# Delta rule: chunk queries and keys weighed together on GpSimd, moments of the outputs on ScalarE

## The chip, the cores and the metric

The kernel runs on one core of a Trainium2 chip. The metric is the time of one execution in microseconds (us) on the device. The engines are TensorE (PE, its weight loads are shown apart as PEld), VectorE (DVE), ScalarE (ACT), GpSimd (POOL) and SyncE (SP), which issues DMAs. Each runs its own list of instructions in order, and they wait for each other through counted semaphores. [...]

## The reference

Four blocks in a row work on x of 8 sequences, 512 tokens and 128 channels, each as x = x + block(layernorm(x)): an attention, an expert layer, the delta rule, and the expert layer again. The change is in the delta rule only:

```python
def step(S, inp):
    qt, kt, vt, at, gkt = inp
    Sp = S * jnp.exp(gkt)[..., None]
    u = jnp.einsum('bhk,bhkv->bhv', at, Sp) + vt
    S = Sp + jnp.einsum('bhk,bhv->bhkv', kt, u)
    o = jnp.einsum('bhk,bhkv->bhv', qt, S)
    return (S, o)
...
out = dplr_delta_rule(q, k, v, a, gk)      # a = k * gamma * exp(gk)
gate = jax.nn.sigmoid(x @ Wg1 @ Wg2)
out = out * gate
mu = jnp.mean(out, axis=-1, keepdims=True)
var = jnp.mean(jnp.square(out - mu), axis=-1, keepdims=True)
out = (out - mu) * jax.lax.rsqrt(var + 1e-05) * norm_w
return out @ Wo
```

There are 16 heads of 8 channels, so 8 sequences times 16 heads are 128 independent recurrences, one per partition.

## The kernel before

The delta rule has four stages on the time axis.

1. Projections (up to about 682 us in the profile): q, k, v, the decay and the gates are made and laid out with one head of one sequence per partition. `Q`, `K`, `V` and `W` are SBUF tiles of 128 x 4096 float32, in the order channel d, place j in the chunk, chunk c. A chunk is `CH` = 8 tokens, and there are `NCH` = 64 chunks. So two neighbouring places of one chunk lie 64 elements (256 bytes) apart, and two channels 512 elements.
2. Tables (about 682 to 758 us): for all chunks at once, VectorE multiplies (`product`), TensorE sums over the channels with an identity matrix (`sums`), and VectorE puts the lower triangular systems together in `LL` and `QQ`. Each product has one of four buffers, so `product(g)` waits for the sums of piece g-4. In between VectorE weighs all keys at once, W = K * beta (L2133), and at the end ScalarE replaces K by the keys that carry a token's part to the end of its chunk (L1933).
3. Recurrence (about 758 to 956 us): 64 chunks one after the other. Per chunk VectorE does four operations, each needing the one before it: the products of the state S with the weighted keys `w_c` (L2198, 128x512), their sum X (L2205), the products of X with the carried keys `k_c` (L2207, 128x512), and their sum, the new S (L2212). S and X lie in PSUM. ScalarE serves (`serve`): it scales the old state, copies S and X to SBUF for GpSimd, and with `fetch` copies the next chunk's decay, keys, values and weighted keys out of the big tiles to small ones, the weighted keys turned to the order j, k so that the channel k lies innermost. GpSimd makes the outputs of the chunk (`outputs`): it weighs the chunk's queries (L1854), multiplies them with S (L1863) and the table QQ with X (L1868). TensorE adds these products up with the identity, four chunks at a time (`add_up`). In the last eight chunks GpSimd also multiplies the first half of the outputs by the gate (L1888, four operations, one after each of the chunks 56 to 59).
4. Tail (about 956 to 984 us): eight units of four tiles of 128 tokens. Per unit TensorE turns the tiles to have the tokens on the partitions (L2376) and multiplies them with the output weights `wo_c` (L2381), VectorE takes mean and variance of the turned tiles (bn_stats L2241, bn_aggr L2245), ScalarE takes the root (L1996), and VectorE takes the reciprocal and adds the scaled result to x (L2253, L2258). The last quarter of the tokens (`ob_c`, units 6 and 7) goes through DRAM to get its layout (L1811, L1820) and is then gated on VectorE (L2235). The expert layer begins after a barrier of all engines.

The order on every engine is the order in which the code is written; there is no scheduler. The stage lines that matter in `chain` of the kernel before are:

```python
k_c = ahead[:, at, 0].rearrange("p (k j) -> p k j", k=HD)
w_c = ahead[:, at, 1].rearrange("p (j k) -> p j k", j=CH)
dve.wait_ge(s["fetched"], c + 1)
dve.wait_ge(s["chain"], n + 1)
dve.tensor_tensor(pu[:, at, :, :, 0:HD], w_c.unsqueeze(1).broadcast_to([P, HD, CH, HD]),
                  S[at].unsqueeze(2).broadcast_to([P, HD, CH, HD]), ALU.mult)
```

## Time and profile before

| what | value |
|---|---|
| median of 3 runs | 1165.15 us (1164.67 to 1171.54) |
| the profiled execution | 1174.14 us, its span 1172.4 us |
| TensorE | busy 878.4 us (75%), mean granted clock 0.82 |
| VectorE | busy 747.8 us (64%) |
| ScalarE | busy 529.9 us (45%) |
| GpSimd | busy 550.5 us (47%) |

A busy share is a mean over stages with different limits, so what a change in one stage is worth has to be read from that stage. The span runs from the first to the last instruction of the profiled execution; the time adds 1.7 us around it. The profiled execution is 9 us above the median.

### The profile page before, as it was taken

Reading aid. Unit: us, or ns where it says so; the run is one execution under the profiler, and the core shown is the slowest. Engines: PE = TensorE matmul, PEld = TensorE weight load, DVE = VectorE, ACT = ScalarE, POOL = GpSimd, SP = SyncE. Lnnn points to the kernel's source line nnn. Section 1 sums busy time; section 2 is a strip of 40 time slices with the busy share of each in tenths; the row PEclk is TensorE's granted clock in tenths of the full one; section 3 lists DMA queues with packets and bytes.
Section 4 is the critical chain, followed back from the end, with each engine's and each line's share of the span. In section 5 each row is a group of like instructions: output and inputs, shape, how many; then the busy total and the mean of one; then the engine's idle time right before and its main releaser. Section 6 shows DMA issues by size and latency. Waiting matters only on the chain. (4 is left out here: it accounts for less than half of the span.)

```text
span 1172.4 us, 26225 instructions
## 1 busy us (share of the span) xinstructions
PE 878.4 (75%) x9192; PEld 620.1 (53%) x9192; DVE 747.8 (64%) x1726; ACT 529.9 (45%) x1212; POOL 550.5 (47%) x685
## 2 busy tenths in 40 slices
PE   3789889898888553799459769877677774629992
PEld 2355464555564453688324367346565563527881
DVE  7476585667775774122374499989999998731223
ACT  4477676677786411345134300255555531104540
POOL 3455555656656346144310000078888860552442
PEclk8597797889997755799769969969888886558996
DMA  5242240422440002667424830000011100126765
GB/s 166 64 153 74 81 150 25 133 88 77 143 148 8 11 28 81 168 193 210 124 68 126 214 69 1 1 0 1 0 36 36 36 19 18 37 87 186 209 194 161
DMA packets 126567, 106.24 MB, mean 91 GB/s; under 512 B 19984, under 2 KB 113872, under 8 KB 126032
## 3 DMA queue, kind: packets, MB, share of 16 engines
q1 hardware_dynamic: 121040, 94.37, 27.8%
q0 software_dynamic: 4992, 10.27, 2.6%
q8 instruction: 67, 1.10, 0.4%
q14 instruction: 36, 0.29, 0.1%
q10 hardware_dynamic: 432, 0.20, 0.1%
HBM read 63.48 MB, written 41.21 MB: 89 GB/s over the span
## 5 line engine op out<-in xcount | busy, mean ns | idle before, releaser
L723 DVE TENSOR_SCALAR a_mag<-a_pS 128x1024 int32<-128x1024 int32 (+1 forms) x192 | 177.7, 948 | 70.9 <-PE a_pS L929 61.5
L504 ACT ACTIVATE a_pw<-a_mag,a_eps_a 128x1024 f32<-128x1024 f32 (+1 forms) x192 | 173.5, 929 | 43.9 <-DVE a_mag L723 41.2
L343 POOL TENSOR_TENSOR a_pw<-a_pw,a_decay 128x256 f32<-128x256 f32 x128 | 93.2, 728 | 131.4 <-ACT a_pw L504 129.3
L1211 POOL DMA_INDIRECT ys_dram<-f_yo,f_who x92 | 88.0, 957 | 128.2 <-DVE f_yo L1476 112.1
L929 PE MATMUL a_pS<-a_qf,a_kf 64*64 64x192 bf16 (+3 forms) x1536 | 109.0, 266 | 13.3 <-DVE a_mag L723 9.9
L1279 ACT ACTIVATE f_hs<-f_bH,f_bias 128x256 f32<-128x256 f32 x184 | 72.1, 474 | 63.8 <-PE f_bH L1574 63.8
L2358 PE MATMUL d_c<-d_pb_p,d_ident 128*128 128x256 f32 x256 | 73.8, 459 | 27.7 <-POOL d_pb_p L1868 27.7
L1203 POOL DMA_INDIRECT xs_dram<-f_xa,f_pos x64 | 61.7, 965 | 64.6 <-DVE f_pos L1396 47.5
L1574 PE MATMUL f_bH<-f_xsT,f_w1s 128*128 128x256 f32 x368 | 91.3, 393 | 0.0
L1464 DVE TENSOR_SCALAR f_ysT<-f_bY,f_bias 128x256 f32<-128x256 f32 x46 | 22.2, 483 | 107.7 <-PE f_bY L1584 106.3
L961 PE MATMUL a_pOff<-a_pw,a_vo 128*18 128x64 f32 x3584 | 88.8, 228 | 1.3 <-issue 1.3
L1584 PE MATMUL f_bY<-f_hs,f_w2s 128*128 128x256 f32 x368 | 87.0, 379 | 0.0
L929 PEld LDWEIGHTS a_pS<-a_qf,a_kf 64*64 64x64 bf16 x1536 | 63.4, 112 | 38.8 <-DVE a_mag L723 12.6
L2358 PEld LDWEIGHTS d_c<-d_pb_p,d_ident 128*128 128x128 f32 x256 | 59.7, 237 | 42.9 <-issue 26.0
L2358 PE MATMUL d_c<-d_pb_d,d_ident 128*128 128x256 f32 (+1 forms) x256 | 63.2, 412 | 21.4 <-POOL d_pb_d L1868 21.4
L1574 PEld LDWEIGHTS f_bH<-f_xsT,f_w1s 128*128 128x128 f32 x368 | 69.4, 199 | 8.3
L1863 POOL TENSOR_TENSOR d_pb_p<-d_qd,d_s_sb 128x512 f32<-128x512 f32 x32 | 34.2, 1068 | 82.8 <-ACT d_s_sb L1963 77.9
L961 PEld LDWEIGHTS a_pOff<-a_pw,a_vo 128*18 128x18 f32 x3584 | 63.0, 102 | 15.9 <-issue 11.4
L1584 PEld LDWEIGHTS f_bY<-f_hs,f_w2s 128*128 128x128 f32 x368 | 66.5, 190 | 7.2
L2358 PEld LDWEIGHTS d_c<-d_pb_d,d_ident 128*128 128x128 f32 x256 | 52.1, 216 | 32.8 <-POOL d_pb_d L1868 24.6
L1854 POOL TENSOR_TENSOR d_qd<-d_Q,d_alpha 128x64 f32 (+1 forms) x64 | 26.3, 411 | 88.5 <-ACT d_alpha L1928 88.5
L291 POOL TENSOR_TENSOR a_vo<-a_vd,a_reach 128x1008 f32<-128x1008 f32 (+6 forms) x56 | 65.8, 1189 | 1.1 <-issue 1.1
(355 smaller groups left out, 1826.3 us busy)
## 6 DMA issues: line engine op xcount, KB each, us to landing
parts_scratch<-a_parts SPq DMA_DIRECT2D x32, 384.0 KB, 3.5
f_w1s<-in_L_ffn_w_dram SPq DMA_DIRECT2D x46, 256.0 KB
f_w2s<-in_L_ffn_w_dram SPq DMA_DIRECT2D x46, 256.0 KB
a_kf<-parts_scratch SPq DMA_DIRECT2D x16, 512.0 KB, 5.2
a_qf<-parts_scratch SPq DMA_DIRECT2D x16, 512.0 KB, 6.2
f_xs<-xs_dram SPq DMA_DIRECT2D x46, 129.0 KB, 2.2
parts_scratch<-a_parts SPq DMA_DIRECT2D x16, 256.0 KB, 2.5
f_ya<-ys_dram SPq DMA_DIRECT2D x16, 256.0 KB, 4.8
```

Source lines behind the costliest of these rows:

```text
L291: pool.tensor_tensor(vo[:, vo_at(j, j + 1):vo_at(j, j + 1) + n, :, :], vd[:, k, j, :, :].unsqueeze(1).broadcast_to([P, n, NP, 18]), reach[ ...
L343: pool.tensor_tensor(own, own, decay[:, k, m, hf:NP:2, :], ALU.mult)\
L504: act.activation(pw[:, n % 4, 0:N], mag[:, n % 3, 0:N], ACT.Square, bias=eps_a[:, 0:1])\
L723: dve.tensor_scalar(mag[:, n % 3, 0:2 * N].bitcast(I32).rearrange("p (l t) -> p l t", l=2), pS[:, 2 * (n % 2):2 * (n % 2) + 2, 0:N].bitcas ...
L929: ins = pe.matmul(pS[lo:hi, 2 * (n % 2) + Q // 2, at:at + L * (end - first)], kf[lo:hi, k, p, L * m:L * m + L], qf[lo:hi, k, p, L * first: ...
L961: ins = pe.matmul(pOff[lo:hi, L * i:L * i + L], vo[:, vo_at(m, i), p, :], wi, start=False, stop=(m == NM - 2), skip_group_check=True)
L1203: pool.indirect_dma_start(xs_dram[f][:, :], bass.IndirectOffsetOnAxis(ap=pos[:, i:i + 1], axis=0), xa[:, i, :], None).then_inc(s["scat_don ...
L1211: pool.indirect_dma_start(ys_dram[f][:, :], bass.IndirectOffsetOnAxis(ap=who[:, q, a:a + 1], axis=0), yo[:, q, a, :], None).then_inc(ys_ou ...
L1279: ins = act.activation(hs[:, q % 2, n, :], bH[:, 2 * (q % 2) + n // 2, ST * (n % 2):ST * (n % 2) + ST], ACT.Gelu, bias=bias[:, q, n:n + 1])
L1574: ins = pe.matmul(bH[:, 2 * (q % 2) + n // 2, ST * (n % 2):ST * (n % 2) + ST], w1s[:, q, P * n:P * n + P], xsT[:, q % 2, :], start=True, s ...
L1584: ins = pe.matmul(bY[:, 0:ST], w2s[:, q, n, :], hs[:, q % 2, n, :], start=(n == 0), stop=(n == NF - 1))
L2358: ins = pe.matmul((c5, c6)[a][:, 0:64 * chunks].rearrange("p (c x) -> p c x", x=64), ident[:, :], po[:, k], start=(k == 0), stop=(k == 15))
```

## The change

- The full weighting of the keys (W = K * beta on VectorE, 128 x 4096) is gone. `Q` and `K` now lie in one tile `QK_both`, `alpha` and `beta` in one tile `weights`, and GpSimd weighs a chunk's 64 query and 64 key elements in one operation of 128x128 (`weigh`), one chunk ahead of its other work. It waits until VectorE and GpSimd have read the buffer's last content.
- The carried keys go to `W` now and `K` stays whole.
- ScalarE's `fetch` has three copies in place of four. VectorE reads the weighted keys where GpSimd puts them, in the order k, j, through a view that has the channel innermost: neighbouring elements are then 8 elements (32 bytes) apart. VectorE waits for GpSimd's weighing besides ScalarE's fetch.
- In the tail a tile is multiplied with [wo_c | I - 1/C] at once (128x256), which gives the mapped tile and the centred tile, tokens on the partitions. ScalarE squares the centred tile with a sum over the channels, then takes the root. The turning matmuls and VectorE's bn_stats and bn_aggr are gone. VectorE gates the last quarter after unit 3 in place of after unit 4.

```diff
-        Q = sb("Q", [P, HD, CH, NCH])
-        K = sb("K", [P, HD, CH, NCH])
+        QK_both = sb("QK_both", [P, 2, HD, CH, NCH])
+        Q, K = QK_both[:, 0], QK_both[:, 1]
-        qd = sb("qd", [P, 2, HD, CH])
+        qw = sb("qw", [P, 2, 2, HD, CH])
-        turned_in = (c4, c1, c3)
-        mapped_in = (c7, c2, c0)
+        mapped_in = ((c4, c7), (c1, c2), (c3, c0))
...
+            def weigh(c, at):
+
+                pool.tensor_tensor(qw[:, at],
+                                   QK_both[:, :, :, :, bass.ds(c, 1)].rearrange("p a k j c -> p a k (j c)"),
+                                   weights[:, :, :].rearrange("p a (j c) -> p a j c", j=CH)[:, :, :, bass.ds(c, 1)]
+                                   .rearrange("p a j c -> p a (j c)").unsqueeze(2).broadcast_to([P, 2, HD, CH]), ALU.mult)\
+                    .then_inc(s["cc_step"], 1)
...
-                pool.tensor_tensor(qd[:, a % 2], Q[:, :, :, bass.ds(c, 1)].rearrange("p k j c -> p k (j c)"),
...
+                if not (isinstance(r, int) and c == NCH - 1):
+                    if not (isinstance(r, int) and c == 0):
+                        pool.wait_ge(s["chain"], 4 * c - 2)
+                        pool.wait_ge(s["po_mul"], 2 * c - 1)
+                    weigh(c + 1, (a + 1) % 2)
+                pool.wait_ge(s["cc_step"], N_CC + 1 + c)
...
-                act.activation(ahead[:, at, 1].rearrange("p (j k) -> p j k", j=CH),
-                               W[:, :, :, bass.ds(c, 1)].rearrange("p d j c -> p j (d c)"), ACT.Copy)\
...
             for u in range(len(UNITS)):
+                act.wait_ge(s["oy_ps"], u + 1)
+                for k in range(4):
+                    ins = act.activation(mapped(u, k)[:, C:2 * C], mapped(u, k)[:, C:2 * C], ACT.Square,
+                                         accum_out=osq[:, 4 * u + k:4 * u + k + 1])
+                ins.then_inc(s["ost_step"], 1)
...
-            dve.tensor_tensor(W[:, :, :, :].rearrange("p d j c -> p d (j c)"), K[:, :, :, :].rearrange("p d j c -> p d (j c)"),
-                              beta[:, :].unsqueeze(1).broadcast_to([P, HD, T]), ALU.mult).then_inc(s["w_step"], 1)
...
-                w_c = ahead[:, at, 1].rearrange("p (j k) -> p j k", j=CH)
+                w_c = qw[:, at, 1].rearrange("p k j -> p j k")
                 dve.wait_ge(s["fetched"], c + 1)
+                dve.wait_ge(s["cc_step"], N_CC + 1 + c)
...
+            for u in range(4):
+                add_in(u)
+            for h in range(2):
+                gated(ob_c, 2, h, 3 * T // 4)
+            for u in range(4, len(UNITS)):
+                add_in(u)
...
-                for k in range(4):
-                    ins = pe.transpose(tp[:, P * k:P * k + P], o_tile(i, 4 * h + k), ident[:, :])
-                ins.then_inc(s["ot_ps"], 1)
...
-                    ins = pe.matmul(yp[:, P * k:P * k + P], o_tile(i, 4 * h + k), wo_c[:, :], start=True, stop=True)
+                    ins = pe.matmul(mapped(u, k), o_tile(i, 4 * h + k), wo_2[:, :], start=True, stop=True)
```

GpSimd, chunks 59 to 61 near the end of the recurrence, before (`d_qd` holds the weighted queries, `d_pb_p` and `d_pb_d` the products, `d_G` the outputs that are being gated; L1888 is the last of the four gatings):

```order
L1854 TENSOR_TENSOR d_qd<-d_Q,d_alpha 128x64
L1863 TENSOR_TENSOR d_pb_p<-d_qd,d_s_sb 128x512 [waits d_act_step,d_cc_step]
L1868 TENSOR_TENSOR d_pb_p<-d_QQ,d_x_sb 128x512 [waits d_act_step]
L1888 TENSOR_TENSOR d_G<-d_G,d_gate 128x512 [waits f_row_in3]
L1854 TENSOR_TENSOR d_qd<-d_Q,d_alpha 128x64
L1863 TENSOR_TENSOR d_pb_d<-d_qd,d_s_sb 128x512 [waits d_sum_ps,d_act_step,d_cc_step]
L1868 TENSOR_TENSOR d_pb_d<-d_QQ,d_x_sb 128x512 [waits d_act_step]
```

The same place now (`d_qw` holds the weighted queries and keys of the chunk that follows):

```order
L1860 TENSOR_TENSOR d_qw<-d_QK_both,d_weights 128x128 [waits d_po_mul,d_chain]
L1880 TENSOR_TENSOR d_pb_p<-d_qw,d_s_sb 128x512 [waits d_act_step,d_cc_step]
L1885 TENSOR_TENSOR d_pb_p<-d_QQ,d_x_sb 128x512 [waits d_act_step]
L1907 TENSOR_TENSOR d_G<-d_G,d_gate 128x512 [waits f_row_in3]
L1860 TENSOR_TENSOR d_qw<-d_QK_both,d_weights 128x128 [waits d_po_mul,d_chain]
L1880 TENSOR_TENSOR d_pb_d<-d_qw,d_s_sb 128x512 [waits d_sum_ps,d_act_step,d_cc_step]
L1885 TENSOR_TENSOR d_pb_d<-d_QQ,d_x_sb 128x512 [waits d_act_step]
```

The places are the same, but the weighing now has 128 elements in place of 64 and belongs to the next chunk, so VectorE's chunk 61 needs the operation that stands behind the last gating and the outputs of chunk 59.

VectorE, units 1 and 2 of the tail, before (`d_c` is PSUM, `d_ost` and `d_omv` the moments, `d_ors` the reciprocal root):

```order
L2241 BN_STATS d_ost<-d_c 128x6 x4
L2245 BN_AGGR d_omv<-d_ost 128x2 x4
L2253 RECIPROCAL d_ors<-d_ors 128x4
L2258 SCALAR_TENSOR_TENSOR x<-d_c,d_ors,x 128x128 x4
L2241 BN_STATS d_ost<-d_c 128x6 x4
L2245 BN_AGGR d_omv<-d_ost 128x2 x4
```

The same engine and place now:

```order
L2261 RECIPROCAL d_ors<-d_ors 128x4
L2266 SCALAR_TENSOR_TENSOR x<-d_c,d_ors,x 128x128 x4
L2261 RECIPROCAL d_ors<-d_ors 128x4
L2266 SCALAR_TENSOR_TENSOR x<-d_c,d_ors,x 128x128 x4
```

The moments have left VectorE; on ScalarE each unit now has four squares of 128x128 (L2014) ahead of its root.

## Rows read from the trace of the kernel before

**Rows 1.** Windows: us, busy of PE, PEld, DVE, ACT, POOL (instructions), PE clock, DMA share, GB/s.

```profile
786.00:930.00 144.00, 104.11 (x384) 84.68 (x384) 137.42 (x190) 80.46 (x347) 123.96 (x145) 0.86 0.07 22
...
972.00:978.00 6.00, 1.81 (x9) 1.82 (x10) 5.26 (x23) 0.37 (x2) 0.00 (x0) 0.63 0.00 0
```

**Rows 2.** Timeline of DVE, one chunk: start us, duration us, engine, line, operation [idle before].

```profile
849.68 0.69 DVE L2198 TENSOR_TENSOR d_og<-d_og,d_c 128x512 f32<-128x512 f32 x1
...
852.71 0.69 DVE L2198 TENSOR_TENSOR d_og<-d_og,d_c 128x512 f32<-128x512 f32 x1
```

**Rows 3.** Timeline of POOL, the same chunk.

```profile
849.41 1.16 POOL L1868 TENSOR_TENSOR d_pb_d<-d_QQ,d_x_sb 128x512 f32<-128x512 f32 x1 [0.21 <-ACT d_x_sb L1971]
850.53 0.41 POOL L1854 TENSOR_TENSOR d_qd<-d_Q,d_alpha 128x64 f32 x1
851.12 1.07 POOL L1863 TENSOR_TENSOR d_pb_d<-d_qd,d_s_sb 128x512 f32<-128x512 f32 x1 [0.17 <-POOL d_qd L1854]
```

**Rows 4.** Groups of DVE by form: count, busy us, mean ns of one, idle before.

```profile
L2228 DVE TENSOR_REDUCE d_LL<-d_pb_d 128x64 f32<-128x1024 f32 x2 | 3.8, 1916 | 0.4 <-POOL d_pb_d L1868 0.4
...
L1393 DVE TENSOR_REDUCE f_pos_f<-f_p_at 128x8 f32<-128x64 f32 x6 | 1.6, 270 | 0.2
...
L1370 DVE TENSOR_REDUCE f_first<-f_hit 128x8 f32<-128x64 f32 x6 | 1.3, 220 | 0.2
...
L1428 DVE TENSOR_REDUCE f_lsum<-f_lgx 128x32 f32<-128x256 f32 x2 | 0.8, 410 | 0.0
```

**Rows 5.** Timelines of DVE and then PE in the table stage.

```profile
689.74 4.41 DVE L2133 TENSOR_TENSOR d_W<-d_K,d_beta 128x4096 f32<-128x4096 f32 x1
...
728.82 2.28 DVE L2065 TENSOR_TENSOR d_pb_d<-d_LL,d_K 128x2048 f32<-128x2048 f32 x1
...
758.28 0.69 DVE L2198 TENSOR_TENSOR d_og<-d_og,d_c 128x512 f32<-128x512 f32 x1 [0.98 <-ACT d_og L1950]
...
710.74 6.32 PE L2334 MATMUL d_c<-d_pb_d,d_ident 128*128 128x256 f32 x32 [1.22 <-DVE d_pb_d L2070]
...
723.80 7.03 PE L2329 MATMUL d_c<-d_pb_d,d_ident 128*128 128x512 f32 x16
```

**Rows 6.** Timeline of DVE, the last sum of chunk 7.

```profile
785.13 0.76 DVE L2212 TENSOR_REDUCE d_c<-d_G 128x64 f32<-128x576 f32 x1 [2.80 <-ACT d_s_sb L1963]
```

**Rows 7.** Timelines of POOL and then DVE at the end of the recurrence.

```profile
946.88 1.28 POOL L1888 TENSOR_TENSOR d_G<-d_G,d_gate 128x512 f32<-128x512 f32 x1
948.11 0.45 POOL L1854 TENSOR_TENSOR d_qd<-d_Q,d_alpha 128x64 f32<-128x64 f32 x1
...
957.55 1.16 POOL L1868 TENSOR_TENSOR d_pb_d<-d_QQ,d_x_sb 128x512 f32<-128x512 f32 x1
...
946.75 0.69 DVE L2198 TENSOR_TENSOR d_og<-d_og,d_c 128x512 f32<-128x512 f32 x1
...
955.05 0.76 DVE L2212 TENSOR_REDUCE d_c<-d_G 128x64 f32<-128x576 f32 x1
```

**Rows 8.** Timelines of DVE and then ACT in the tail, and SP's reload of the last quarter.

```profile
970.45 0.88 DVE L2241 BATCH_NORM_STATS2 d_ost<-d_c 128x6 f32<-128x128 f32 x4
...
971.91 1.12 DVE L2258 SCALAR_TENSOR_TENSOR x<-d_c,d_ors,x 128x128 f32<-128x128 f32 x4
972.95 0.88 DVE L2241 BATCH_NORM_STATS2 d_ost<-d_c 128x6 f32<-128x128 f32 x4
...
962.36 1.28 ACT L1996 ACT_TABLE_LOAD   x1
...
967.52 0.94 SPq L1820 DMA_DIRECT2D d_fg<-o_dram  x2
```

**Rows 9.** Timeline of ACT at the program's start: squares of 128x128 with a sum.

```profile
5.40 0.31 ACT L430 ACTIVATE a_sq<-a_wn 128x128 f32<-128x128 f32 x1 [2.21 <-DMA a_wn<-in_L_attn_a_W_dram]
...
5.71 0.29 ACT L431 ACTIVATE a_dia_sb<-a_wn 128x128 f32<-128x128 f32 x1
```

**Rows 10.** Chain that ended last, expert layer: four float32 matmuls of 128x256 in 8 passes.

```profile
1065.87 1.73 PE f_bH L1574 x8
```

More of the change, by code:

```diff
@@ L1875, in _ @@
             pool.wait_ge(q_in, q_in_0 + 32)
+            pool.wait_ge(k_in, k_in_0 + 48)
+            weigh(0, 0)
             for a in range(8):
@@ L2235, in gated @@
                 dve.tensor_tensor(t[:, b4, :], t[:, b4, :], gate[:, b4, at:at + P], ALU.mult).then_inc(og_done[1], 1)
-            def moments(u):
-                tp = turned_in[u % 3]
-                dve.wait_ge(s["ot_ps"], u + 1)
-                for k in range(4):
-                    ins = dve.bn_stats(ost[:, 4 * u + k, :], tp[:, P * k:P * k + P])
-                ins.then_inc(s["stat_done"], 1)
-                dve.wait_ge(s["stat_done"], 2 * NT + u + 1)
-                for k in range(4):
-                    ins = dve.bn_aggr(omv[:, 4 * u + k, :], ost[:, 4 * u + k, :])
-                ins.then_inc(s["ost_step"], 1)
             def add_in(u):
                 i, h = UNITS[u]
-                yp = mapped_in[u % 3]
                 at = slice(4 * u, 4 * u + 4)
@@ L2263, in _ @@
             last_sum(2)
-            moments(0)
             last_sum(3)
@@ L2267, in _ @@
                 gated(ob_b, 1, h, T // 2)
-            for u in range(1, len(UNITS)):
-                if u == 6:
-                    for h in range(2):
-                        gated(ob_c, 2, h, 3 * T // 4)
-                moments(u)
-                add_in(u - 1)
-            add_in(len(UNITS) - 1)
+            for u in range(4):
[4 more added lines that the diff above has]
+                add_in(u)
         @block.tensor
@@ L2373, in map_unit @@
                 if u >= 3:
[L2374 removed]
+                    pe.wait_ge(s["ost_done"], u - 2)
+                if u == 0:
+                    pe.wait_ge(s["c_consts"], 2)
                 for k in range(4):
[L2376 to L2381 removed]
+                    ins = pe.matmul(mapped(u, k), o_tile(i, 4 * h + k), wo_2[:, :], start=True, stop=True)
                 ins.then_inc(s["oy_ps"], 1)
```

52 lines of the change are left out of this document (24 added, 28 removed).

## The prediction

> **What bounds the kernel now.** I read the windows first, then each engine's timeline in the four stages that the change touches, and last the groups by form, for prices. In the recurrence VectorE is busy 137 of 144 us, GpSimd 124, ScalarE 80 [rows 1]. The timeline of one chunk shows why: VectorE's four operations follow each other without idle time, and the first of them comes again after 852.71 - 849.68 = 3.03 us [rows 2]. Nothing else paces these 64 chunks, so whatever lengthens one of the four by x costs 64 x. GpSimd's three operations take 1.16 + 0.41 + 1.07 = 2.64 us of that, with two short waits [rows 3]: it has about 0.4 us to spare. ScalarE has more. Ahead of the recurrence VectorE runs without gaps, and TensorE nearly so. In the tail VectorE is the pace: a unit every 972.95 - 970.45 = 2.50 us [rows 8].
>
> **The term that decides: VectorE's read of the weighted keys.** Before, ScalarE's fetch laid them with the channel innermost, so the first multiplication read neighbours. Now it reads the same 64 values (eight times over, 512 elements) with 32 bytes between neighbours. The trace has no multiplication that reads SBUF so, but two reductions that do. `place` sums 64 elements over an axis with 32 bytes between neighbours (L1393) and takes 270 ns, where the same shape read in order (L1370) takes 220: 0.78 ns more per element. `last_sum` reads 1024 elements 256 bytes apart (L2228) in 1916 ns. In order, 64 elements take 220 and 256 take 410, so 0.99 ns per element, and 1024 would take 1170: the extra is 746 / 1024 = 0.73 ns per element [rows 4]. So the price does not hang on how large the stride is, and applies in either row. On 512 elements it makes 0.37 to 0.40 us, and the multiplication 0.69 would become about 1.07. The bound below is zero: only one of the two operands (the other, S, is PSUM and in order) is strided, and a multiplication may hide what a reduction shows. I take 0.375 us, since both rows agree though shapes and strides differ widely: 64 x 0.375 = **+24 us**. It lies wholly on the path, because each of the four operations waits for the last.
>
> The Trainium skill, Advanced Engine Details and Errata, section SBUF Cachelines, says that SBUF is read in lines of 16 bytes and that an access pays when it does not hit the line of the one before, at least two hits per line being needed. It names no operation, so by it the multiplication pays as the reduction does, and the sum stays as it is here; it gives no size, and no row here shows a multiplication.
>
> **GpSimd's weighing.** It grows from 64 to 128 elements. Below: 0.41 plus 64 elements at the slope between 64 and 512 elements, (1.07 - 0.41) / 448 = 1.5 ns each, is 0.50 us. Above: twice the operation, 0.82. Both operands are strided as before, so I take the middle, 0.66 [rows 3]. It is no longer followed by a wait for itself (the 0.17 us ahead of L1863), since the products read what was weighed a chunk earlier. So the products would start about where they do now: 0.66 in place of 0.41 + 0.17. GpSimd needs 0.66 + 1.07 + 1.16 = 2.89 us a chunk, below 3.03, and far below 3.4: nothing. The new waits ahead of it (VectorE's first multiplication of the chunk before and GpSimd's own products) are over long before; behind the weighing stand GpSimd's two products, and VectorE waits for it. That wait is met about 1.5 us early in the steady part: weighing for the chunk at 852.71 would end at 851.2. VectorE's additional wait is one more instruction that its queue passes while a 0.76 us sum runs. ScalarE's fetch loses a copy of 0.2 us at issue, off the path except once, ahead of chunk 0.
>
> **The end of the recurrence.** Here the lead is gone. With four gatings of 1.28 us, GpSimd works without a gap and is behind: it weighs for chunk 60 at 948.11, while VectorE had started chunk 61 already at 946.75 [rows 7]. In the new order that place weighs for chunk 61, and ends near 948.7, 1.9 us after VectorE wants it. At the old chunk time VectorE would so lose about 2.4 us over chunks 57 to 63 in all. At 3.4 us a chunk GpSimd falls behind less, and the loss is about 1.0. Against this, the work after it starts with GpSimd's last product, which ended at 958.71, 2.9 us after VectorE's last sum (955.05 + 0.76) [rows 7]; in a slower chain it ends only some 1 us after it. Net 0, from -1 to +1.5. In the same way the stall of 2.80 us in chunk 7 [rows 6], where ScalarE waits for a gate from TensorE behind the first four chunks' sums, shrinks: the sums start 4 x 0.375 later, the chain is 8 x 0.375 later there: **-1.5**.
>
> **The table stage.** The full weighting, 4.41 us, had no idle time around it. If TensorE followed, all of it would go. But products wait for TensorE's sums of four pieces earlier, and TensorE has only 1.22 us idle until late in the stage. I carried both engines' durations through the slots: VectorE is free 4.41 us sooner until the product that stood at 728.82, which would start at 724.4. It needs the sums of piece 12, the first half of the 7.03 us at 723.80, moved ahead by 1.22: 723.80 - 1.22 + 3.44 = 726.0. So 1.6 us come back as a wait, after it nothing is late: -2.8. With the first fetch shorter by 0.2 of its 0.98 us it is **-3** (from -4.6 if TensorE's slots never bind, to -1.2, TensorE's idle time alone) [rows 5].
>
> **The tail.** VectorE loses 0.88 us of bn_stats and about 0.4 of bn_aggr a unit, and keeps about 1.4. TensorE needs 1.73 us for four matmuls of 128x256 at full clock [rows 10]. ScalarE: squares with a sum follow at 0.31 [rows 9], so 4 x 0.31, some 0.2 for the last sum's readout, 0.1 of waiting and 0.3 for the root: 1.8 us a unit, the new pace. It starts with the squares (1.4) and then the table load (1.28) that stood at 962.36 [rows 8], so the first root comes at 965.4, seven more units take 12.6, the last addition 1.4: 979.4, where the additions now end at 983.8. That is -4.4. The last quarter comes back some 3 us after SyncE's issue at 967.5 [rows 8], in time for the gating after unit 3, which VectorE has room for. If TensorE's clock is low for the last two units, as it was at 972 to 978 (0.63) [rows 1], they take up to 3.5 us each and 3 us of the gain are lost. **-4**, from -5.5 to -1.
>
> **Sum.** +24 - 3 - 1.5 + 0 - 4 = +15.5 us on 1174.14 of the profiled execution, in which no term scales with the 9 us that it lies above the median. On 1165.15: **1180.5 us**, +1.3%. About 1% is what a measurement of this kernel can tell from no change. With the bounds of its terms (22.5 to 26 for the read) this case spans 1175 to 1187.
>
> **Rivals.** (A) The multiplication hides the strided read: both operands stream at one element per cycle whatever the stride. For it: no such multiplication is in the trace, and ScalarE's strided copies are not visibly slower. Against it: two reductions that pay alike. Then -3, stall unchanged, +2.4 at the end of the chain less some 1.5 that the tail had waited for GpSimd anyway, -4 to -5: about -6, **1159 us**. It decides as soon as the multiplication stays under about 0.75 us. This is the side that is not slower.
> (B) GpSimd becomes the pace: the weighing at 0.82, and the 0.17 us of issue time stay, since in the loop its waits are computed in registers: 0.82 + 0.17 + 1.07 + 1.16 = 3.22 us. Against it: no idle shows ahead of L1854 in the loop, so its queue runs ahead. Under the forecast's 3.4 it is hidden; with A it costs 64 x 0.19 = 12: **1171 us**.
> (C) The tail gains nothing, TensorE at low clock being the pace at up to 3.5 us: +4 on the forecast, **1184.5**, within its range.
>
> **Chances.** Forecast with or without C 0.68, A 0.25, B 0.07. The forecast's low end is just at +1%, A's far end just beyond -1%. So faster by over 1% 0.04, within 1% 0.33, slower by over 1% 0.63. The range takes in A: 1157 to 1187; without A, 1175 to 1187.
>
> **What the profile after would show.** The first multiplication of a chunk at 1.05 to 1.09 us and a chunk time of 3.40 to 3.43; the other three unchanged; GpSimd's weighing 0.5 to 0.82 and idle waiting for ScalarE's copies; VectorE waiting for the weighing only in the last eight chunks; the table stage some 3 us shorter with one wait of about 1.6 for TensorE; tail units at 1.8 us with ScalarE the pace. Wrong I am if the multiplication stays at 0.69 (then A), or if GpSimd never waits in the loop (then B).

## The result and the profile after

| | median, us (runs) | ratio to before, 95% interval |
|---|---|---|
| before, on this chip | 1168.35 (1164.67 to 1177.81) | |
| changed | 1181.28 (1176.32 to 1190.53) | 1.0142 [1.0081, 1.0203] |

The changed kernel is slower by 1.4%; forecast were 1180.5 us and +1.3%. Ratios, here and below, are estimates that leave out the slowest executions of a kernel; they differ a little from the ratio of the medians, which is 1.0111 here, inside the interval.

The profiled execution takes 1178.30 us, 4.2 more than that of before, while the medians are 12.9 apart. The reason is the part ahead of the change. It differs from execution to execution, whatever the kernel: the first key sum starts at 681.9 us before, at 674.9 here, at 659.8 to 690.0 in the experiments. So I compare stages by their own lengths and not whole profiles. I cut at four places of VectorE's timeline: its first operation with the key sums, its first multiplication of the recurrence, the end of its last sum there, and the first operation of the expert layer. For the kernel after these rows are (timeline of VectorE):

```profile
674.88 1.28 DVE L2137 TENSOR_TENSOR d_LL<-d_c,d_LL 128x512 f32<-128x512 f32 x2
...
746.52 1.07 DVE L2218 TENSOR_TENSOR d_og<-d_qw,d_c 128x512 f32<-128x512 f32 x1 [0.79 <-ACT d_og L1968]
...
967.91 0.76 DVE L2232 TENSOR_REDUCE d_c<-d_G 128x64 f32<-128x576 f32 x1
...
988.20 0.87 DVE L1329 BATCH_NORM_STATS2 f_stats<-x 128x6 f32<-128x128 f32 x4 [0.33 <-PEq L1623]
```

All kernels of this study, cut in the same way (us, but the last column in ns, the median of the recurrence's first multiplication; the differences are of the unrounded lengths):

| kernel | tables | recurrence | tail | sum | against before | first mult. |
|---|---|---|---|---|---|---|
| before | 76.3 | 197.5 | 28.3 | 302.2 | | 687 |
| after | 71.6 | 222.2 | 19.5 | 313.3 | +11.1 | 1084 |
| e1_stride_alone | 76.4 | 221.2 | 27.3 | 324.8 | +22.6 | 1080 |
| e2_in_order | 73.1 | 200.1 | 21.7 | 294.8 | -7.4 | 686 |
| e3_weigh_earlier | 73.2 | 202.7 | 23.0 | 298.9 | -3.3 | 686 |
| e4_tail_alone | 76.4 | 197.5 | 24.2 | 298.0 | -4.2 | 686 |
| e5_weighting_back | 76.1 | 221.7 | 19.6 | 317.5 | +15.3 | 1082 |
| e6_stride_8_bytes | 76.4 | 196.0 | 27.8 | 300.1 | -2.1 | 686 |
| e7_stride_16_bytes | 76.4 | 220.2 | 27.3 | 323.9 | +21.7 | 1070 |
| e8_four_buffers | 71.7 | 197.9 | 23.0 | 292.6 | -9.6 | 686 |
| e9_root_table_early | 73.2 | 200.1 | 20.4 | 293.7 | -8.5 | 686 |
| e10_both | 71.8 | 197.9 | 21.7 | 291.4 | -10.8 | 686 |
| e11_both_again | 73.2 | 198.7 | 22.1 | 294.0 | -8.2 | 687 |

Behind the tail 188.3 us are left before and 187.5 after. The three stages hold nearly the whole difference that the change makes: +24.6 in the recurrence, -4.7 in the tables, -8.8 in the tail.

**The recurrence.** The timeline of VectorE for one chunk, as [rows 2]:

```profile
851.23 1.09 DVE L2218 TENSOR_TENSOR d_og<-d_qw,d_c 128x512 f32<-128x512 f32 x1
852.36 0.76 DVE L2225 TENSOR_REDUCE d_c<-d_og 128x64 f32<-128x576 f32 x1
853.15 0.69 DVE L2227 TENSOR_TENSOR d_G<-d_og,d_c 128x512 f32<-128x512 f32 x1
853.88 0.76 DVE L2232 TENSOR_REDUCE d_c<-d_G 128x64 f32<-128x576 f32 x1
854.67 1.08 DVE L2218 TENSOR_TENSOR d_og<-d_qw,d_c 128x512 f32<-128x512 f32 x1
```

Only the first operation has changed, from 0.69 to 1.09 us. It comes again after 3.44 us in place of 3.03, without idle time. GpSimd in the same chunk, as [rows 3]:

```profile
850.97 1.16 POOL L1885 TENSOR_TENSOR d_pb_d<-d_QQ,d_x_sb 128x512 f32<-128x512 f32 x1 [0.40 <-ACT d_x_sb L1988]
852.08 0.63 POOL L1860 TENSOR_TENSOR d_qw<-d_QK_both,d_weights 128x128 f32 x1
852.93 1.07 POOL L1880 TENSOR_TENSOR d_pb_d<-d_qw,d_s_sb 128x512 f32<-128x512 f32 x1 [0.21 <-ACT d_s_sb L1980]
```

The weighing takes 0.63 us, the wait for itself is gone from the loop, and GpSimd waits for ScalarE's copies, 0.40 and 0.21 us in a chunk: it is not the pace. At the two special places VectorE shows these rows; the first answers to [rows 6], the others are all its waits for the weighing:

```profile
774.95 0.76 DVE L2232 TENSOR_REDUCE d_c<-d_G 128x64 f32<-128x576 f32 x1 [1.08 <-ACT d_s_sb L1980]
...
954.46 1.07 DVE L2218 TENSOR_TENSOR d_og<-d_qw,d_c 128x512 f32<-128x512 f32 x1 [0.34 <-POOL d_qw L1860]
...
958.41 1.08 DVE L2218 TENSOR_TENSOR d_og<-d_qw,d_c 128x512 f32<-128x512 f32 x1 [0.56 <-POOL d_qw L1860]
```

The stage adds up: 64 x (1.084 - 0.687) = 25.4, the stall of chunk 7 from 2.80 to 1.08 is -1.7, the two waits are +0.9. That makes +24.6.

The stall of chunk 7 is not the same in all executions of one work. e6_stride_8_bytes does what the kernel before does, with the same chunk time of 3.03 us, and has 1.22 us there in place of 2.80:

```profile
786.06 0.76 DVE L2213 TENSOR_REDUCE d_c<-d_G 128x64 f32<-128x576 f32 x1 [1.22 <-ACT d_s_sb L1964]
```

In the nine profiles with a chunk of about 3.03 us the stall is 1.22 to 2.80 us, in the four with the slower read 0.67 to 1.09. Within the nine it goes with the clock that TensorE had early in the table stage (see "The full weighting put back"): 1.22 to 1.86 us in the three with 0.95 or more there, 2.55 to 2.80 in the six with 0.84 or less. All four with the slower read had 0.93 or more. So like with like the slower chain takes off 0.1 to 1.2 us (0.8 between the means), and the rest of the 1.7 belongs to the execution.

**The tail.** VectorE's timeline, as [rows 8]: the last sums, the gating, then units of a reciprocal and an addition.

```profile
968.58 3.76 DVE L2248 TENSOR_REDUCE d_LL<-d_pb_d 128x64 f32<-128x1024 f32 x2
972.25 1.29 DVE L2255 TENSOR_TENSOR d_G<-d_G,d_gate 128x512 f32<-128x512 f32 x2
973.69 0.18 DVE L2261 RECIPROCAL d_ors<-d_ors 128x4 f32<-128x4 f32 x1
973.97 1.12 DVE L2266 SCALAR_TENSOR_TENSOR x<-d_c,d_ors,x 128x128 f32<-128x128 f32 x4
...
975.43 1.13 DVE L2266 SCALAR_TENSOR_TENSOR x<-d_c,d_ors,x 128x128 f32<-128x128 f32 x4
...
986.74 1.13 DVE L2266 SCALAR_TENSOR_TENSOR x<-d_c,d_ors,x 128x128 f32<-128x128 f32 x4
```

The first units follow at 975.43 - 973.97 = 1.46 us, where 2.50 stood before. Over all eight it is (986.74 - 973.97) / 7 = 1.82. Who paces the later ones is seen on TensorE and ScalarE:

```profile
956.53 8.78 PE L2364 MATMUL d_c<-d_pb_p,d_ident 128*128 128x256 f32 x32 [5.63 <-POOL d_pb_p L1885]
965.15 1.89 PE L2383 MATMUL d_c<-d_wo,d_G 128*128 128x256 f32 x8
966.87 3.73 PE L2364 MATMUL d_c<-d_pb_d,d_ident 128*128 128x128 f32 x32
...
975.24 5.42 PE L2383 MATMUL d_c<-d_wo,d_G 128*128 128x256 f32 x24 [1.18 <-DVE x L2266]
```

```profile
972.06 1.28 ACT L2018 ACT_TABLE_LOAD   x1
973.36 0.30 ACT L2018 ACTIVATE d_ors<-d_osq,d_eps_ln 128x4 f32<-128x4 f32 x1
...
977.24 0.26 ACT L2014 ACTIVATE d_c<-d_c 128x128 f32<-128x128 f32 x1 [0.67 <-PE d_c L2383]
```

ScalarE's own pace is 974.82 - 973.36 = 1.46 us a unit (its roots follow so), as long as TensorE has mapped ahead. From the fourth unit on ScalarE waits for TensorE, which maps at 5.42 / 3 = 1.81 us a unit. It could begin the fourth only when VectorE's first addition had freed one of the three places in PSUM (the 1.18 us in its row). TensorE has the full clock here, 1.00 in the column behind the five busy times, where a granted clock of 1.00 is full speed (the second row answers to the last of [rows 1]; the first to its first):

```profile
786.00:930.00 144.00, 100.48 (x330) 80.49 (x329) 138.19 (x168) 62.31 (x263) 118.06 (x127) 0.75 0.04 15
972.00:978.00 6.00, 4.82 (x23) 3.96 (x22) 5.43 (x18) 5.24 (x27) 0.00 (x0) 1.00 0.47 140
```

### The profile page after: what moved, and what is told of

Read it like the earlier page. It is cut to its first block and busy times, and to the rows that moved or that the text cites. A ratio compares the mean times of both kernels' runs of the same rounds, so it can differ in the third digit from the quotient of the medians.

```text
span 1175.7 us, 26219 instructions
## 1 busy us (share of the span) xinstructions
PE 880.4 (75%) x9160; PEld 622.8 (53%) x9160; DVE 760.1 (65%) x1661; ACT 526.1 (45%) x1212; POOL 564.6 (48%) x686
## 3 DMA queue, kind: packets, MB, share of 16 engines
q8 instruction: 66, 1.08, 0.4%
## 5 line engine op out<-in xcount | busy, mean ns | idle before, releaser
L2364 PE MATMUL d_c<-d_pb_p,d_ident 128*128 128x256 f32 x256 | 76.9, 474 | 29.5 <-POOL d_pb_p L1885 29.5
L2364 PE MATMUL d_c<-d_pb_d,d_ident 128*128 128x256 f32 (+1 forms) x256 | 71.5, 451 | 26.3 <-POOL d_pb_d L1885 26.3
L2364 PEld LDWEIGHTS d_c<-d_pb_p,d_ident 128*128 128x128 f32 x256 | 61.9, 246 | 45.6 <-issue 27.8
L1860 POOL TENSOR_TENSOR d_qw<-d_QK_both,d_weights 128x128 f32 (+1 forms) x64 | 40.1, 627 | 88.2 <-ACT d_weights L1947 88.2
L2364 PEld LDWEIGHTS d_c<-d_pb_d,d_ident 128*128 128x128 f32 x256 | 58.2, 240 | 40.1 <-POOL d_pb_d L1885 29.5
L1880 POOL TENSOR_TENSOR d_pb_p<-d_qw,d_s_sb 128x512 f32<-128x512 f32 x32 | 34.2, 1067 | 78.9 <-ACT d_s_sb L1980 78.6
L2218 DVE TENSOR_TENSOR d_og<-d_qw,d_c 128x512 f32<-128x512 f32 x64 | 69.3, 1083 | 4.1 <-POOL d_qw L1860 0.9
L961 PEld LDWEIGHTS a_pOff<-a_pw,a_vo 128*18 128x18 f32 x3584 | 62.5, 102 | 15.5 <-issue 10.8
```

The costliest lines, as they stand in the source:

```text
L961: ins = pe.matmul(pOff[lo:hi, L * i:L * i + L], vo[:, vo_at(m, i), p, :], wi, start=False, stop=(m == NM - 2), skip_group_check=True)
L2364: ins = pe.matmul((c5, c6)[a][:, 0:64 * chunks].rearrange("p (c x) -> p c x", x=64), ident[:, :], po[:, k], start=(k == 0), stop=(k == 15))
```

## The experiments

### The stride by itself

Two lines of the kernel before are changed. ScalarE fetches the weighted keys in the order k, j, and VectorE reads them as the changed kernel does; nothing else moves.

```diff
-                act.activation(ahead[:, at, 1].rearrange("p (j k) -> p j k", j=CH),
-                               W[:, :, :, bass.ds(c, 1)].rearrange("p d j c -> p j (d c)"), ACT.Copy)\
+                act.activation(ahead[:, at, 1].rearrange("p (k j) -> p k j", k=HD),
+                               W[:, :, :, bass.ds(c, 1)].rearrange("p d j c -> p d (j c)"), ACT.Copy)\
-                w_c = ahead[:, at, 1].rearrange("p (j k) -> p j k", j=CH)
+                w_c = ahead[:, at, 1].rearrange("p (k j) -> p j k", k=HD)
```

> The kernel before with one edit: ScalarE's fetch leaves the weighted keys in the order k, j, and VectorE reads them with 32 bytes between channels. GpSimd, the table stage and the tail are as before. Theory 1 (each element that VectorE reads 32 bytes from the one before costs about 0.77 ns more): the first multiplication goes from 0.687 to 1.08 us, the chunk from 3.03 to 3.43 us, the recurrence by 25 us, ratio to before 1.02. Theory 2 (the multiplication got longer because it reads a tile that GpSimd has just written and is reading at the same time): it stays at 0.69 us, ratio 1.00.

Measured: 1201.13 us (1192.83 to 1206.25), before on that chip 1174.29; ratio 1.0237 [1.0157, 1.0318]. The first multiplication over all chunks (count, shortest, median and longest in ns):

```profile
L2198 DVE TENSOR_TENSOR d_og<-d_og,d_c x64: 1070/1080/1095, 760.1 to 977.9; 128x512 f32<-128x512 f32 x64
```

The stage of 221.2 us is 23.6 longer than before, the tables and the first multiplication's neighbours are as they were. The tail is only 1.1 us shorter, though GpSimd ends 0.8 us after the chain here too; e4_tail_alone comes back to this. No tile of GpSimd's is read here, so theory 2 is out. The stride is enough for the whole loss, and more: without the gains of the change the kernel is slower than the changed one.

### The weighed keys in order

The changed kernel, but GpSimd writes the channel innermost; the strided access goes to GpSimd (its write, and its read of the queries in the first product).

```diff
-        qw = sb("qw", [P, 2, 2, HD, CH])
+        qw = sb("qw", [P, 2, 2, CH, HD])
-                pool.tensor_tensor(qw[:, at],
+                pool.tensor_tensor(qw[:, at].rearrange("p a j k -> p a k j"),
-                                   qw[:, a % 2, 0].unsqueeze(3).broadcast_to([P, HD, CH, HD]),
+                                   qw[:, a % 2, 0].rearrange("p j k -> p k j").unsqueeze(3).broadcast_to([P, HD, CH, HD]),
-                w_c = qw[:, at, 1].rearrange("p k j -> p j k")
+                w_c = qw[:, at, 1]
```

> The changed kernel with the weighed queries and keys laid in the order j, k, so that VectorE reads the keys in order; GpSimd still makes and reads them. Theory 1: the first multiplication is back at 0.69 us and the chunk at 3.03 to 3.06 us, if GpSimd keeps up; its weighing and its product with S now have the stride, 0.63 to 0.70 and 1.07 to 1.16 us, 2.97 us a chunk in all. In the last eight chunks VectorE then waits 2.5 to 4 us in all for the weighing. Against before: -4.4 in the table stage, +3 at the end of the recurrence, -6 to -8 in the tail, ratio 0.993. Theory 2: the multiplication stays near 1.08 us, ratio 1.014 as the changed kernel.

Measured: 1165.76 us (1145.76 to 1180.01), before 1174.29 (1163.77 to 1186.53), ratio 0.9943 [0.9894, 0.9993]. The multiplication is back at 686 ns and the chunk at 3.03; the other parts of the change leave a gain of 7.4 us in the stages. (The profiled execution is the fastest of the ten, 20 us under their median; what is short in it is the part ahead of the key sums, and the stages are like those of e9_root_table_early.) GpSimd's product with the queries has grown from 1.07 to 1.17 us. GpSimd works without a gap at the end and falls behind, and VectorE waits three times:

```profile
915.80 0.69 DVE L2218 TENSOR_TENSOR d_og<-d_qw,d_c 128x512 f32<-128x512 f32 x1 [0.71 <-POOL d_qw L1860]
...
919.83 0.69 DVE L2218 TENSOR_TENSOR d_og<-d_qw,d_c 128x512 f32<-128x512 f32 x1 [1.02 <-POOL d_qw L1860]
...
923.88 0.69 DVE L2218 TENSOR_TENSOR d_og<-d_qw,d_c 128x512 f32<-128x512 f32 x1 [1.04 <-POOL d_qw L1860]
```

That is 2.8 us, the loss that the prediction put at 2.4 for "the old chunk time". In the table stage VectorE waits once, which it doesn't in the kernel after:

```profile
703.61 2.29 DVE L2087 TENSOR_TENSOR d_pb_d<-d_LL,d_QK_both 128x2048 f32<-128x2048 f32 x1 [1.39 <-PE d_c L2335]
```

### The weighing two chunks ahead, two buffers

The same, and `weigh(c + 2)` stands between GpSimd's two products, so that it is done before GpSimd can fall behind. It goes into the buffer whose queries the product just issued has read, so it waits for that product.

```diff
-                    weigh(c + 1, (a + 1) % 2)
...
                     .then_inc(s["po_mul"], 1)
+                if not (isinstance(r, int) and c >= NCH - 2):
+                    pool.wait_ge(s["chain"], 4 * c + 2)
+                    pool.wait_ge(s["po_mul"], 2 * c + 1)
+                    weigh(c + 2, a % 2)
                 pool.wait_ge(s["act_step"], 3 * c + 3)
```

> The kernel of e2_in_order with the weighing two chunks ahead, between GpSimd's two products, and so ahead of the gatings. If VectorE's waits in the last chunks come from the weighing standing behind a gating (theory 1), they go, and the recurrence is 2.5 to 4 us shorter than in e2_in_order, ratio to before 0.990. If GpSimd is simply too slow with the wider weighing (theory 3), the chunk in the steady part is above 3.06 us here as in e2_in_order, and the waits stay.

Measured: 1173.83 us (1156.34 to 1179.84), and no ratio is on record. Theory 1 fell. GpSimd's timeline of a chunk shows why:

```profile
851.05 1.17 POOL L1875 TENSOR_TENSOR d_pb_d<-d_qw,d_s_sb 128x512 f32<-128x512 f32 x1
852.41 0.65 POOL L1860 TENSOR_TENSOR d_qw<-d_QK_both,d_weights 128x128 f32 x1 [0.19 <-POOL d_pb_d L1875]
853.01 1.16 POOL L1884 TENSOR_TENSOR d_pb_d<-d_QQ,d_x_sb 128x512 f32<-128x512 f32 x1
854.13 1.16 POOL L1875 TENSOR_TENSOR d_pb_d<-d_qw,d_s_sb 128x512 f32<-128x512 f32 x1
```

It works without a gap but for 0.19 us ahead of the weighing, where it waits for its own product, and comes round after 854.13 - 851.05 = 3.08 us. That is 0.05 more than VectorE's 3.03, so it falls further behind from chunk to chunk. VectorE keeps its 3.03 us up to about chunk 40 and goes at 3.07 from there on, which costs it only 0.5 us over the loop. But with no lead left, the four gatings at the end are paid almost in full: VectorE waits 1.25, 1.22, 1.21 and 1.23 us there, 4.9 in all. This is rival B of the prediction in small, where the stride doesn't cover it.

### The new tail alone

The kernel before with the tail of the changed one: `wo_2` with the centring matrix, the maps of 128x256, ScalarE's squares with their sum, and VectorE's `add_in`.

```diff
+            pool.tensor_tensor(center, ident[:, :], ones[:, :], ALU.subtract).then_inc(s["c_consts"], 1)
...
             for u in range(len(UNITS)):
+                act.wait_ge(s["oy_ps"], u + 1)
+                for k in range(4):
+                    ins = act.activation(mapped(u, k)[:, C:2 * C], mapped(u, k)[:, C:2 * C], ACT.Square,
+                                         accum_out=osq[:, 4 * u + k:4 * u + k + 1])
...
-            def moments(u):
```

> The kernel before with the new tail alone (matmuls with both matrices at once, squares on ScalarE, no moments on VectorE, last quarter gated after unit 3). From the last sum of the chain (955.8 in before) to the expert layer's first operation (984.1) it is 28.3 us before and 19.5 us in the changed kernel. If the new tail is what gives all of the 8.8 us, it is 19.5 here too. If a part comes from GpSimd, which ends 2.9 us after the chain before and 0.8 us after it in the slower chain of the changed kernel, it is 21.5 to 23.5 here. Ratio to before 0.993 to 0.996.

Measured: 1172.45 us (1156.93 to 1182.04), ratio 0.9949 [0.9897, 1.0]. The tail takes 24.2 us in the one execution that was profiled, 4.2 less than before, but 4.6 more than in the changed kernel, with the same code, and more than the 21.5 to 23.5 expected. What differs is when it can start. TensorE here:

```profile
953.00 10.12 PE L2354 MATMUL d_c<-d_pb_p,d_ident 128*128 128x256 f32 x32 [5.62 <-POOL d_pb_p L1873]
962.95 1.89 PE L2373 MATMUL d_c<-d_wo,d_G 128*128 128x256 f32 x8
964.68 3.73 PE L2354 MATMUL d_c<-d_pb_d,d_ident 128*128 128x128 f32 x32
```

The chain ends at 961.85. TensorE is through with the sums of the chunks 56 to 59 (the first row) only at about 963, and its last sums (the row at 964.68) end 6.6 us after the chain. In the changed kernel the same three rows, shown above, end 970.60 - 968.67 = 1.9 us after it. The difference is the 4.6 of the tail, and it has two parts. The first group starts 12.1 us ahead of the chain's end in the changed kernel and 8.9 here (3.3), because GpSimd is less late against a slower chain: it ends 0.8 us after the chain in place of 2.9. And the group takes 8.78 us in place of 10.12 (1.3); TensorE's granted clock over the last 9 us of the chain was 0.99 there and 0.66 here.

In the kernel before TensorE was as late as here:

```profile
946.98 10.15 PE L2358 MATMUL d_c<-d_pb_p,d_ident 128*128 128x256 f32 x32 [5.59 <-POOL d_pb_p L1868]
...
958.30 3.74 PE L2358 MATMUL d_c<-d_pb_d,d_ident 128*128 128x128 f32 x32
```

But there it cost next to nothing: VectorE, the pace of the old tail, waited 0.37 us for GpSimd and 0.16 for TensorE ahead of its second unit. That is why the slower chain by itself shortens the tail by 1.1 us only (e1_stride_alone), the new tail by itself by 4.2, and both together by 8.8. The new tail has little work on VectorE, and so the end of TensorE's sums decides when it starts.

### The full weighting put back

The changed kernel with VectorE's full weighting of the keys in its old place, its result unused.

```diff
-            wn = 0
+            dve.wait_ge(s["knorm_step"], 2)
+            dve.tensor_tensor(W[:, :, :, :].rearrange("p d j c -> p d (j c)"), K[:, :, :, :].rearrange("p d j c -> p d (j c)"),
+                              beta.unsqueeze(1).broadcast_to([P, HD, T]), ALU.mult).then_inc(s["w_step"], 1)
+            wn = 1
```

> The changed kernel with the full weighting of the keys put back on VectorE, its result overwritten and unused, so that only its time counts. From the first key sums (674.9 in the changed kernel) to the first multiplication of the chain (746.5) the changed kernel takes 71.6 us, the kernel before 76.3. If the 4.4 us operation is on the path in full, this takes 76.1. If TensorE's slots hid a part, as the prediction's 1.6 us of wait, it takes about 74.5.

Measured, one execution: 1194.88 us. The table stage is 76.1 against 71.6: 4.5 us for this operation:

```profile
693.71 4.42 DVE L2155 TENSOR_TENSOR d_W<-d_QK_both,d_weights 128x4096 f32<-128x4096 f32 x1
```

So in the kernel after the weighting's removal had counted in full, and TensorE's slots took nothing back. In e2_in_order and e3_weigh_earlier they took back 1.39 and 1.52 us. Windows of ten microseconds, begun some 5 us after TensorE has started on the tables, say what was different. The kernel after, then e2_in_order, then before:

```profile
683.00:693.00 10.00, 10.00 (x56) 9.25 (x56) 9.90 (x10) 0.00 (x0) 0.00 (x0) 0.98 0.00 0
```

```profile
667.00:677.00 10.00, 10.00 (x49) 9.54 (x49) 9.90 (x10) 0.00 (x0) 0.00 (x0) 0.79 0.00 0
```

```profile
690.00:700.00 10.00, 10.00 (x48) 9.46 (x48) 9.80 (x8) 0.00 (x0) 0.00 (x0) 0.82 0.00 0
```

TensorE has the high clock (2.4 GHz) nearly throughout in the first and is partly at the low one (1.2 GHz) in the other two, after an idle stretch of 17.1 us in all three. With the high clock it makes 55 or 56 matmuls in 10 us where it else makes 48 or 49, and VectorE never catches it. Of the seven executions without the weighting three have a granted clock of 0.97 or 0.98 there, no wait, and a stage of 71.6 to 71.8 us; four have 0.79 to 0.84, one wait of 1.39 to 1.52 us, and 73.1 to 73.2. Which comes is a matter of the execution: e10_both and e11_both_again are one kernel and have one each.

This also bears on the main comparison. The profile after had the high clock and the one before had not. e6_stride_8_bytes does the work of the kernel before with 0.95 there, and its stages take 300.1 us; against that the changed kernel's 313.3 are +13.2, near the +12.9 of the medians.

### How large a stride

The kernel before, its weighted keys fetched into a tile with room behind each element: 8 bytes from one to the next, and 16.

```diff
+        wide = sb("wide", [P, 2, CH, HD, 2])
-                act.activation(ahead[:, at, 1].rearrange("p (j k) -> p j k", j=CH),
+                act.activation(wide[:, at, :, :, 0],
-                w_c = ahead[:, at, 1].rearrange("p (j k) -> p j k", j=CH)
+                w_c = wide[:, at, :, :, 0]
```

> The kernel before with the fetched weighted keys spread to 8 bytes between channels, in a tile of their own. Theory 1 as the prediction put it (the price does not hang on how large the stride is): the first multiplication takes 1.08 us. If neighbours within 16 bytes cost nothing: 0.69 us.

> As e6_stride_8_bytes with 16 bytes between channels. Each element lies in another 16 bytes than the one before: 1.04 to 1.08 us if the price is full from there on, 0.69 us if it starts above 16 bytes.

Measured, one execution each: 1176.59 and 1206.67 us, before on that chip 1170.36. The multiplication, 8 bytes and then 16:

```profile
L2199 DVE TENSOR_TENSOR d_og<-d_wide,d_c x64: 686/686/689, 760.8 to 953.7; 128x512 f32<-128x512 f32 x64
```

```profile
L2199 DVE TENSOR_TENSOR d_og<-d_wide,d_c x64: 1054/1070/1102, 766.4 to 983.2; 128x512 f32<-128x512 f32 x64
```

At 8 bytes nothing is paid, at 16 nearly all: 1070 against 1080 at 32. The Trainium skill, Advanced Engine Details and Errata, section SBUF Cachelines, has lines of 16 bytes and asks for two hits in each; 8 bytes between float32 elements give two and 16 give one, so the runs agree with it. From 16 to 32 bytes the price hardly grows (1.01 times). Where between 8 and 16 bytes it begins, and whether at once, is not shown; 12 was not run.

### Four buffers, and the root's table early

First, e3_weigh_earlier with four buffers, so that the weighing between the products waits for a product two chunks old:

```diff
-        qw = sb("qw", [P, 2, 2, CH, HD])
+        qw = sb("qw", [P, 4, 2, CH, HD])
+                if not (isinstance(r, int) and c >= NCH - 2):
+                    if not (isinstance(r, int) and c < 2):
+                        pool.wait_ge(s["chain"], 4 * c - 6)
+                        pool.wait_ge(s["po_mul"], 2 * c - 3)
+                    weigh(c + 2, (a + 2) % 4)
```

> The weighed keys in order, and the weighing two chunks ahead, between GpSimd's two products, into four buffers, so that it waits for nothing that GpSimd has just issued. Theory: with two buffers (e3_weigh_earlier) the 0.19 us per chunk in front of the weighing was its wait for GpSimd's own product just ahead; with four it is gone, a chunk takes GpSimd .60 + 1.12 + 1.12 = 2.84 us and no longer sets the pace, the chunk is back at VectorE's 3.03, and the waits for the weighing (2.8 us in e2_in_order, 4.9 in e3_weigh_earlier) fall under 1 us: recurrence 197.5 to 198.5 us against 200.1 and 202.8. From key sums to the expert layer 293 to 295, since GpSimd's total work up to its last product is what it was in e2_in_order and the tail gives back part. Rival: it is the place between the products that costs (ScalarE's copy for the second product, or ports), then the recurrence stays above 200 and the 0.19 us stays.

Measured, one execution: 1163.08 us, before on that chip 1168.18; recurrence 197.9, stages 292.6 (expected 197.5 to 198.5 and 293 to 295). GpSimd's rows:

```profile
849.30 1.17 POOL L1875 TENSOR_TENSOR d_pb_d<-d_qw,d_s_sb 128x512 f32<-128x512 f32 x1
850.41 0.65 POOL L1860 TENSOR_TENSOR d_qw<-d_QK_both,d_weights 128x128 f32 x1
851.00 1.17 POOL L1885 TENSOR_TENSOR d_pb_d<-d_QQ,d_x_sb 128x512 f32<-128x512 f32 x1
852.42 1.17 POOL L1875 TENSOR_TENSOR d_pb_p<-d_qw,d_s_sb 128x512 f32<-128x512 f32 x1 [0.26 <-ACT d_s_sb L1981]
```

The 0.19 is gone, and GpSimd waits for ScalarE again. VectorE's waits for the weighing are 0.29 and 1.05 us, 1.3 in all, a little over the 1 us expected. The rival (the place costs) is out. Against e2_in_order the waits are 1.4 us less, but the tail is 1.3 us longer (23.0 against 21.7), since GpSimd's last product now ends 2.3 us after the chain in place of 0.9. What else is shorter, 1.4 us in the tables and 0.7 in the stall of chunk 7, goes with the high clock of this execution (0.98 in the window of the tables).

Second, e2_in_order with one root of one number between ScalarE's last two copies of outputs, where it waits for TensorE:

```diff
             keep_out(NCH // 8 - 1, 0)
+            act.activation(spare[:, :], eps_ln[:, :], ACT.Sqrt)
             keep_out(NCH // 8 - 1, 1, chunks=2)
```

> The weighed keys in order (e2_in_order), and one root of one number on ScalarE between its last two copies of outputs, where it waits 4.4 us for TensorE, so that the table of the root is loaded there. Theory: the load of 1.28 us leaves the way to the first root, VectorE's wait in front of its first reciprocal falls from 2.3 to about 1.0 us and the tail from 21.7 to about 20.4 us. Rival: the tail is bound by TensorE's last sums and its maps, and the units catch up anyway: then the tail stays within 0.4 us of 21.7. Second rival: the squares load a table of their own, and the load only moves: no gain.

Measured, one execution: 1165.38 us. The load has moved into the wait, and VectorE's first reciprocal waits 1.04 us:

```profile
954.82 1.28 ACT L2011 ACT_TABLE_LOAD   x1
```

```profile
960.98 0.18 DVE L2263 RECIPROCAL d_ors<-d_ors 128x4 f32<-128x4 f32 x1 [1.04 <-ACT d_ors L2020]
```

In e2_in_order it had waited 2.32. The tail is 20.4 against 21.7, the whole load. Neither rival held.

Both together, timed twice, each time with twelve executions:

> Both of the above together: four buffers with the weighing two chunks ahead, weighed keys in order, and the root's table early. From key sums to the expert layer about 292 to 293.5 us against 302.2 before, if each does what is expected; timed: about 1160 us, ratio to before about 0.991 with an interval of +/- 0.005. If the tail only gives back what the recurrence gains, 294 to 295 and a ratio near 0.994, as for e2_in_order.

> The kernel of e10_both once more, since there the stages between key sums and expert layer were 10.7 us shorter than before while twelve timed runs said only 0.997 [0.993, 1.001]. If the stages tell the gain and the rest of the program only scatters, the stages read 71.7 to 73.2, 198 and 21 to 23 us again and the ratio comes out between 0.989 and 0.995. If something outside these stages takes the gain back, the ratio stays at 0.997 or above, and the time ahead of the key sums or behind the tail is longer than before in the profile too.

| | median, us | before, us | ratio, 95% interval |
|---|---|---|---|
| e10_both | 1167.32 (1152.05 to 1171.41) | 1168.18 (1160.06 to 1183.14) | 0.997 [0.993, 1.0011] |
| e11_both_again | 1172.27 (1162.24 to 1178.85) | 1183.40 (1166.27 to 1187.38) | 0.9979 [0.993, 1.0028] |

The stages are 10.8 and 8.2 us shorter than before, the first a little more than expected. Compared within one clock, the four buffers gain nothing: e11_both_again (0.84 in the window of the tables) takes 294.0 us and e9_root_table_early (0.83), with two buffers and the weighing one chunk ahead, 293.7. The recurrence is 1.4 shorter and the tail 1.7 longer. The 2.6 us between e10_both and e11_both_again are the execution. So what brings the stages below the kernel before is the weighting's removal, the new tail and the early table, once the read is in order again. The time shows less. It is clearly below the changed kernel's (1.0142 [1.0081, 1.0203]), but a gain over the kernel before isn't shown, though the medians point to one the second time. By the last expectation's second branch the rest of the program should then be longer. In the profiles it is 867.6 and 873.0 us, against 870.2 before, which is neither. So that question stays open: either the rest gets longer by some 6 us in the mean of executions and two profiles don't show it, or the measurement misses it, with executions of one kernel that lie up to 34 us apart (e2_in_order).

## Why the prediction was right, step by step

- **The term that decides.** Forecast +24 us, from 0.375 us for 512 elements. Measured 0.397, which makes +25.4; e1_stride_alone shows that nothing else of the change is needed for it. The forecast took the price from two reductions, at 0.78 and 0.73 ns per element. The multiplication pays (1084 - 687) / 512 = 0.78. So one strided operand of two is enough, though the other is PSUM and in order: rival A (1159 us) is out, and its bound "stays under about 0.75 us" was far from being met. One sentence was too wide: "the price does not hang on how large the stride is" holds from 16 to 256 bytes (0.75, 0.78 and, for the reduction, 0.73 ns) and fails at 8.
- **GpSimd's weighing.** Forecast 0.66 in the middle of 0.50 to 0.82, measured 0.63. The chunk needs 0.63 + 1.07 + 1.16 = 2.86 us, forecast 2.89. It waits in the loop, so rival B didn't come. e3_weigh_earlier shows that B is no idle threat: 0.19 us of waiting for itself suffice to make GpSimd slower (3.08 us) than VectorE at 3.03, and VectorE is held to 3.07 from about chunk 40 on. The rival's reason for that time (waits computed in registers) was wrong; e8_four_buffers keeps those and loses the 0.19.
- **The stall of chunk 7.** Forecast -1.5, measured -1.7. That this agrees is partly luck: like with like the slower chain takes off 0.1 to 1.2 us, and the rest goes with the execution.
- **The end of the recurrence.** Forecast waits of about 1.0 us, measured 0.9, and GpSimd's last product 0.8 us after the chain, forecast about 1. At the old chunk time 2.4 were forecast, e2_in_order has 2.8.
- **The table stage.** Forecast -3, measured -4.7, 0.1 past the end of its bounds at which TensorE's slots never bind. The wait of 1.6 us did not come after, but did in four other executions (1.39 to 1.52 us). It goes with TensorE's clock in the ten microseconds shown above, and the forecast had carried over TensorE's durations of before, where that clock was 0.82. The mechanism was right, its price belongs to an execution and not to the kernel; -3 is right for the slower value (73.1 to 73.2, that is -3.1 to -3.2).
- **The tail.** Forecast -4, bounds -5.5 to -1, measured -8.8. This is the one term clearly outside its bounds. By itself the new tail gives -4.2 (e4_tail_alone). What was mis-sized is the step "Net 0" of the end of the recurrence: it set GpSimd's earlier end against the waits, but left out TensorE. Before, TensorE took 10.15 us for the sums of the chunks 56 to 59, at partly low clock, and its last sums ended 6.2 us after the chain; after, 1.9. In the old tail VectorE was the pace and this lateness hardly showed; the new tail would have paid for it, and the slower chain spared it that. So with the new tail 4.6 us of the strided read's 25.4 came back (with the old one 1.1). The tail's pace was also put on the wrong engine in its second half: ScalarE alone makes a unit in 1.46 us (1.8 was forecast; the last readout and the root overlap the squares), and TensorE's 1.81 is the pace from the fourth unit on. The mean of 1.82 came out as the forecast's 1.8. Rival C did not come: the clock was 1.00 where it had been 0.63. TensorE is busy 4.82 of these 6 us, where it had been 1.81 of 6.
- **The sum.** +15.5 was forecast. The stages give +11.1, the medians +12.9, the ratio +16.6 with 9.5 to 23.7 as interval. Two terms came out larger as gains (-1.7 and -4.8), the read larger as a loss (+1.4), and the waits at the end (+0.9) stand in the recurrence, where the forecast had set them off at net 0. That the median of 1181.28 lies 0.8 us from the forecast's 1180.5 is luck: the median before was 1165.15 when the forecast was made and 1168.35 with one more execution. The forecast's own terms add to 1180.65, and their upper bounds to 1189, not 1187. The sign rested on the one term that was six times the next, and that one was priced from rows.

## What to carry to other kernels

When a layout is turned so that one engine's write becomes easy, look for the reader on the path and count its elements: here 0.78 ns for each, 64 times 512 of them, against an operation of 4.4 us that was saved once. Turn the access on an engine that has slack instead: with GpSimd doing the strided part the stages were 7.4 us shorter than before and not 11.1 longer. And where GpSimd waited for its own preceding operation it paid some 0.2 us each time. A second pair of buffers removed that, but the waits that it saved VectorE came back in the tail.

The cost of a slower critical chain is less than its length if other engines were late at its end; the gain of a faster one is less for the same reason. So the terms of neighbouring stages do not simply add (-1.1 and -4.2 by themselves were -8.8 together), and the stage behind has to be carried with the new end times of every engine that feeds it. And before two profiles are compared by a few microseconds, look whether TensorE had the same clock in the stage: one kernel, profiled twice, differed by 2.6 us in the three stages.
